# Loading the first four conditions from memory by SP, the row by ScalarE, and sharing the first squares by group

## The reference

```
w      = cond_w[cond]                         # 128 batches, a 32 x 32 matrix of a table of 200 for each
h      = einsum('bct,bcd->bdt', x, w)         # x is 128 x 32 x 256: "conditioning"
logits = h @ gate_w ; top 2 of 8 summed       # scale of a row
y      = square(relu(h @ up_w)) @ down_w + (h @ expert_w) * (sum of the top 2 logits)
out    = x + layernorm(y) * gamma + beta
```

## Time and profile before

| what | value |
|---|---|
| median of three runs | 230.84 us |
| the profiled execution, in all | 230.09 us |
| its span, first to last instruction | 228.5 us |
| TensorE matmul busy | 221.8 us |
| VectorE, ScalarE, GpSimd busy | 162.2, 105.7, 130.5 us |
| granted TensorE clock | 1.0 of full in every slice |
| DMA over the span | 11.81 MB, 52 GB/s |

### The profile page before, as it was taken

The page is one execution under the profiler, slowest core; times in us unless marked ns, Lnnn a source line. Parts: engine busy times, 40 slices in busy tenths (PEclk is TensorE's granted clock), DMA queues, the critical chain, the costliest instruction groups (busy, mean ns, idle before and its releaser), DMA issues.

```text
span 228.5 us, 3998 instructions
## 1 busy us (share of the span) xinstructions
PE 221.8 (97%) x1260; PEld 191.9 (84%) x1260; DVE 162.2 (71%) x352; ACT 105.7 (46%) x187; POOL 130.5 (57%) x131
## 2 busy tenths in 40 slices
PE   7999999999999999999999999999999999999992
PEld 2888888988898888888888888888888888888892
DVE  6486975877667877667677766587766766777884
ACT  3378944444455355444545435534454444444000
POOL 3748776575536663656555664366555575557411
PEclk9999999999999999999999999999999999999999
DMA  3867123030503011000200002000020002000021
GB/s 98 239 205 227 41 68 102 8 99 7 185 11 98 9 43 53 0 0 3 92 0 0 3 0 95 0 3 0 0 95 1 0 0 71 25 0 0 19 99 69
DMA packets 17177, 11.81 MB, mean 52 GB/s; under 512 B 6660, under 2 KB 16900, under 8 KB 17156
## 3 DMA queue, kind: packets, MB, share of 16 engines
q1 hardware_dynamic: 15460, 10.43, 15.2%
q10 hardware_dynamic: 1280, 1.07, 1.5%
q0 software_dynamic: 416, 0.05, 0.2%
HBM read 7.35 MB, written 4.19 MB: 51 GB/s over the span
## 4 chain that ended last, share of the span: by engine, by line
PE 93%; DVE 2%; DMA 1%; issue 1%; ACTq 1%; ACT 0%; DVEq 0%
PE up_ps L337 38%; PE down_ps L431 25%; PE down_ps L433 13%; PE hid_ps L303 5%; PE moe_ps L447 3%; PE moe_ps L449 3%; PE moe_ps L448 3%; DMA wd<-in_L_cond_weights_dram 1%; ACTq L513 1%; PE down_ps L303 1%; DVE up_lo L619 1%; DMA cond_row<-in_itok_B_dram 1%; PE down_ps L429 0%; PE down_ps L427 0%; PE down_ps L428 0%
## 5 line engine op out<-in xcount | busy, mean ns | idle before, releaser
L677 POOL TENSOR_TENSOR sq_lo<-square,sq_hi 128x512 fp32r<-128x512 f32 x64 | 83.6, 1310 | 78.6 <-DVE square L552 77.4
L431 PE MATMUL down_ps<-down_hl,sq_hi 128*128 128x512 f32 x248 | 88.8, 393 | 0.0
L433 PE MATMUL down_ps<-down_hl,sq_lo 128*128 128x256 f32 x248 | 69.6, 280 | 0.0
L552 DVE SCALAR_TENSOR_TENSOR square<-up_ps,relu 128x512 f32<-128x512 f32 x64 | 43.8, 686 | 35.7 <-ACT relu L491 26.2
L431 PEld LDWEIGHTS down_ps<-down_hl,sq_hi 128*128 128x128 f32 x248 | 46.5, 188 | 10.8 <-issue 0.3
L491 ACT ACTIVATE relu<-up_ps 128x512 f32<-128x512 f32 x64 | 38.1, 595 | 33.5 <-PE up_ps L337 33.5
L337 PE MATMUL up_ps<-hid_hi,up_hi 128*128 128x512 f32 (+1 forms) x136 | 52.8, 391 | 0.7 <-ACT hid_hi L476 0.3
L337 PE MATMUL up_ps<-hid_hi,up_lo 128*128 128x512 f32 (+1 forms) x136 | 51.1, 379 | 0.0
L433 PEld LDWEIGHTS down_ps<-down_hl,sq_lo 128*128 128x128 f32 x248 | 46.7, 188 | 2.4
L493 ACT ACTIVATE sq_hi<-relu 128x512 fp32r<-128x512 f32 x64 | 40.5, 633 | 2.0
L337 PE MATMUL up_ps<-hid_lo,up_hi 128*128 128x512 f32 (+1 forms) x136 | 40.6, 381 | 0.0
(11 more groups left out here) (62 smaller groups left out, 195.6 us busy)
## 6 DMA issues: line engine op xcount, KB each, us to landing
x_sb<-in_x_dram SPq DMA_DIRECT2D x7, 512.0 KB, 4.3
out_dram<-result SPq DMA_DIRECT2D x7, 512.0 KB, 3.1
wd<-in_L_cond_weights_dram SPq DMA_DIRECT2D x111, 4.0 KB, 1.6
x_sb<-in_L_ffn_down_w_dram SPq DMA_DIRECT2D x2, 512.0 KB, 4.4
x_sb<-in_x_dram ACTq DMA_DIRECT2D x2, 256.0 KB, 3.0
result<-in_L_ffn_up_w_dram ACTq DMA_DIRECT2D x2, 256.0 KB, 2.9
result<-in_L_ffn_up_w_dram SPq DMA_DIRECT2D x1, 512.0 KB, 4.6
out_dram<-result SPq DMA_DIRECT2D x4, 128.0 KB, 1.7
```

The lines of the kernel that those rows point to most:

```text
L431: pe.matmul(dst[:, :], a_hi, down_hl[:, c, :, :].rearrange("p s t -> p (s t)"), start=(c == 0), stop=False)
L433: mm = pe.matmul(dst[:, T:2 * T], a_lo, down_hl[:, c, 0, :], start=False, stop=(c == CH - 1))
L552: dve.scalar_tensor_tensor(square[:, c % 2, :], up_ps[c % UPB][:, :], 0.0, relu[:, c % 2, :], ALU.max, ALU.mult).then_inc(square_done, 1)
L677: pool.tensor_tensor(sq_lo[:, j % 2, c, :], square[:, c % 2, :], sq_hi[:, j % 2, c, :].bitcast(f32), ALU.subtract).then_inc(sq_lo_done, 1)
```

## The change

The four squares of group 0 (batches 0 to 3) are now all issued by SP, those of group 1 (4 to 7) all by ScalarE. SP no longer waits for the row in SBUF: it loads the conditions of batches 0 to 3 into registers straight from the input tensor in memory. It waits for the row only before it loads the values of batches 8 to 15. ScalarE issues both parts of the row, the first ahead of x and the second behind the first up weights, and loads 4 values in place of 8.

```diff
-BY_SP, BY_ACT, BY_POOL, BY_SP_LATER = (0, 2, 4, 6), (1, 3, 5, 7), (8, 9, 10, 11, 12), (13, 14, 15)
+BY_SP, BY_ACT, BY_POOL, BY_SP_LATER = (0, 1, 2, 3), (4, 5, 6, 7), (8, 9, 10, 11, 12), (13, 14, 15)
...
         def conditions(engine, batches):
+            return registers(engine, cond_row[0:1, batches.start:batches.stop], batches)
+
+        def registers(engine, row, batches):
             _, values = nc.values_load_multi_w_load_instructions(
-                cond_row[0:1, batches.start:batches.stop], [engine],
+                row, [engine],
                 skip_runtime_bounds_check_because="a condition is an index into the table by the kernel's contract")
             return dict(zip(batches, values))
...
-            cond_flat = cond.rearrange("(o b) -> o b", o=1)
-            sp.dma_start(cond_row[:, 0:TILES * Q], cond_flat[:, 0:TILES * Q]).then_inc(cond_first_landed, 16)
-            sp.dma_start(cond_row[:, TILES * Q:ROWS_B], cond_flat[:, TILES * Q:ROWS_B]).then_inc(cond_later_landed, 16)
-            sp.wait_ge(cond_first_landed, 16)
-            values = conditions(mybir.EngineType.SP, range(0, HALF_BLOCK))
+
+            values = registers(mybir.EngineType.SP, cond_flat[0:1, BY_SP[0]:BY_SP[-1] + 1], BY_SP)
             sp.wait_ge(wd_zeroed[0], 1)
             for b in BY_SP:
                 sp.dma_start(square_of(b), weights_of(values[b])).then_inc(wd_first_landed[b // Q], 16)
+            sp.wait_ge(cond_first_landed, 16)
             values = conditions(mybir.EngineType.SP, range(HALF_BLOCK, 2 * HALF_BLOCK))
...
             act.activation(table_loaded[:, :], nc.const_aps.tensor(0.0, [P, 1], f32), ACT.Copy)
+            act.dma_start(cond_row[:, 0:TILES * Q], cond_flat[:, 0:TILES * Q]).then_inc(cond_first_landed, 16)
             load_x_first(act, 0)
             load_up(act, 0)
+            act.dma_start(cond_row[:, TILES * Q:ROWS_B], cond_flat[:, TILES * Q:ROWS_B]).then_inc(cond_later_landed, 16)
             act.wait_ge(cond_first_landed, 16)
-            values = conditions(mybir.EngineType.Activation, range(0, HALF_BLOCK))
+            values = conditions(mybir.EngineType.Activation, range(BY_ACT[0], BY_ACT[-1] + 1))
             act.wait_ge(wd_zeroed[0], 1)
```

More of the change, by code:

```diff
@@ L220, in weights_of @@
             return cond_w[bass.ds(row, 1), :, :].rearrange("s c d -> (s c) d")
+        cond_flat = cond.rearrange("(o b) -> o b", o=1)
         def load_up(queue, part):
```

## The result

The changed kernel takes 230.97 us (median of 22 runs, 230.63 to 231.44) against 230.50 of the kernel before on the same chips (22 runs, 230.11 to 231.0). The ratio is 1.0020, 95% interval 1.0012 to 1.0027: 0.47 us slower, 0.28 to 0.62. The forecast was 231.0 and "no change, +0.16". The time of 231.0 is met, but in part by its base: I had added to 230.84, the median of three runs, and that of 22 is 230.50. The loss itself is 0.47 and not 0.16, just past the 0.46 that I had called a change.

What follows compares the result with a forecast made beforehand. TensorE's matmuls bound the kernel, busy 221.8 of 228.5 us, with 0.09 to win at the head. Group 1 +0.08, weights +0.05 and bandwidth +0.05 gave +0.2 profiled; 230.84 + 0.16 gave 231.0, 8 in 10 within 230.3 to 231.6.

Steps and rivals of the forecast that it cites:

- the 0.46: Whole run: 0.2%, 0.46 us, was taken as the least difference that can be told from no change.
- SP's load: Head, SP: 4 values from memory in 1.20 us, there at 2.12; first square at about 2.29, 0.76 earlier.
- first rival: SP ahead of group 0: slow load from memory, over 0.46 late from 1.75 us; 231.6 or 234.3; chance 0.12.
- Group 0: Head: four squares in a row on SP, last landing at 5.3 to 5.6; first matmul moves by up to 0.1.
- ScalarE's queue: Head: two row issues more, a shorter load; first square of group 1 at 3.24 against 3.06, 0.18 later.
- the 7.3: Head, TensorE: a start of group 1 past 7.3 would show the prediction wrong; 6.7 to 7.0 was expected.
- second rival: Head: ScalarE's queue is the new bound, group 1 +0.45; 0.45 to 0.65 slower in all, 231.4; chance 0.14.
- The floor: Head, TensorE: constants until 5.88, then group 0, so group 1 not before 6.72; at most 0.09 us to win.
- SP's list: Behind SP's squares: load_up(2) issued 0.77 earlier, worth nothing; may take bandwidth from other transfers, nothing to 0.3.
- second gap: TensorE behind its start: 0.3 us, ends with VectorE's list; moves with the head and is not closed.
- third rival: Timed runs: SP's lead of 0.77 gives back up to 0.7 where its transfer is late, 230.2; chance 0.17.
- The sum: Whole run: group 1 +0.08, second quarter of weights +0.05, bandwidth +0.05; together +0.2, no change, chance 0.57.

Runs made afterwards that it cites:

- e6: Changed kernel with both issues of the condition row back on SP, ahead of its load from memory: 233.84 us against 230.51, ratio 1.0143.
- e2: Kernel before with only the row moved: ScalarE issues both parts, sharing of squares unchanged, values from SBUF: 231.32 us against 230.34, ratio 1.0036.
- e7: Changed kernel with the old alternating sharing of squares, SP loading 8 values from memory, ScalarE 8 from SBUF: 231.05 us against 230.51, ratio 1.0029.
- e1: Kernel before with only the split: SP issues squares 0 to 3, ScalarE 4 to 7: 230.60 us against 230.34, ratio 1.0010.
- e3: Kernel before, expert and gate weights rounded behind the first chunk, their low part behind the first square: 230.72 us against 230.34, ratio 1.0004.
- e8: Kernel before with e3's moves and the first down weights rounded behind chunk 4 instead of 3: 230.15 us against 230.51, ratio 0.9985.
- e9: Changed kernel with the same moves as e8: 230.31 us against 230.32 for the kernel before, ratio 1.0006.
- e11: Kernel before with squares 0, 1, 6, 7 on SP and 2 to 5 on ScalarE: 230.99 us against 230.32, ratio 1.0032.
- e12: Kernel before with the sharing of e11 and the moves of e8: 230.20 us against 230.32, ratio 0.9993.

## Why the prediction was right, and where not

- **SP's load.** I took 1.20 us for one load, and it is two, 1.40 together with the hand-over: first square 2.50, not 2.29. That there is an address to fetch first, I had not thought of. L stayed below the 1.75 of the first rival; e6, where the two loads take 2.3 behind the two issues of the row, shows what that rival would have been: +3.33 us.
- **Group 0.** "The last lands at 5.3 to 5.6." It was issued at 4.12, not 3.80, and took 2.2 to land, now that SP's squares go out right behind ScalarE's first transfers (the landings of all four are the row below): group 0 from 6.45 instead of 5.88.

```profile
DMA to landing us min/median/max: 2.2/2.2/2.7
```

This is the step that failed: I took the landing time of squares issued from 3.05 on (1.5 to 1.8 of the earlier trace rows) for squares issued from 2.50. The runs between bear it out: 1.6 to 2.0 from 3.09 in e2, 1.9 to 2.3 from 2.90 in e7, with ScalarE's two large issues where the changed kernel has them. The four in a row count by themselves too. In e1 they start at 3.06 and land within 1.9, and group 0 starts at 6.62, because the last is issued at 4.60. The changed kernel issues its last square 0.48 earlier than e1 and starts group 0 only 0.17 earlier; the longer landing takes back the rest.

- **ScalarE's queue.** I had 3.24 with ends of 3.16 and 3.60; it is 3.62. Each of three terms was a little small: 0.51 and 0.35 for the row's issues where SP had needed 0.37 and 0.24, and 0.58 for the load of 4 where I took 0.38. Group 1 came at 7.43, past the 7.3 at which I had said I would be wrong. The second rival, 0.14, was the truer one on the head, with its +0.45 for group 1 against +0.62.
- **The floor.** I held 5.88 for the end of the constants. In e3 and e8 group 0 starts at 5.60, and the changed kernel's own constants end at 5.52. I also took 0.42 for group 0's second pair of matmuls, which takes 0.22 in e1 (6.92 to 7.14). So the head had more than 0.09 to give. It was not the reason why nothing was gained.
- **SP's list.** I had "an earlier landing is worth nothing" and up to 0.3 for bandwidth. It lands 1.24 later, and the second gap "moves with the head, and is not closed" grew by 0.6 in the profile. I had looked at SP's transfer and not at what ScalarE's late ones do to it.
- **The third rival** (SP's lead is worth something): no sign of it. The kernel before does have runs up to 231.5. e3's profile, of that length, loses its time where VectorE meets GpSimd near 18.7; no long run of the kernel before was profiled.
- **The sum.** +0.2 came out as +0.47, though the profile holds 0.6 and 0.6. The head is worth about 0.5 by e9 against e8. It may be that what the changed kernel loses in its second gap, the kernel before loses elsewhere in part of its runs, near 18.7 for one place. That is argued from the spread of the runs and from e3; no run shows it instruction by instruction, and why the two 0.6 come out as 0.47 stays open. By the bound of 0.46 the result stands on the line between "no change" and my 0.26 for slower. So the time was right with a head that was wrong by 0.5 us (+0.62 for group 1, not +0.08) and with a base that was 0.34 too high. That is luck, and no proof of the reasoning.

## What to carry over

A chain through two queues is only as early as the fuller one: count what each issue ahead of a wait costs on the queue it is moved to, and take landing times from a stretch that is as busy as the new one. A transfer can land later though it is issued earlier, as `load_up(2)` did here (issued 0.27 earlier, landed 1.24 later), so look at what shares the DMA engines with it. Before a gain of some tenths is looked for at the head, take away the stalls that come and go from run to run, since they are worth as much: here the first down weights, rounded behind chunk 4 instead of 3, gave 0.29 us, which no single wait in the traces accounts for.

## What the runs showed of the hardware

- A register load from an input tensor is two: its address, 0.86 us at 0.9 us into the run and 1.74 at 1.6 beside large transfers, and 0.51 us for 4 values or 0.91 for 8.
- A load of 4 values from SBUF took 0.50 to 0.58 us from the fifth value of the row on, and 1.11 and 1.12 from the third (e11, e12); 8 values from the first took 0.72 to 0.83. I don't know why.
- VectorE's subtraction of 128x512 with both inputs in SBUF took 1.73 us instead of 0.77 when it started behind one of GpSimd's, and GpSimd's took 1.76 instead of 1.30 in the other order (e3, the kernel before).
- After 2.7 us without a matmul TensorE's granted clock was 0.5 in every window from 10 to 13 us (e6).
